# Two-layer cross-attention on one core: the first layer's scores go from one 96-row bf16 product per head to two heads in two 64-row tiles

## The reference, cut to what matters

```
q, k, v = x @ Wq + bq, ctx @ Wk + bk, ctx @ Wv + bv    # q: 32 heads of 16; k, v: 8 heads of 16
scores  = q_head . k_head * 16 ** -0.5 + mask          # 512 x 1024 for each of 32 heads
out     = softmax(scores) @ v_head
x       = layer_norm(x + out @ Wo + bo) * gamma + beta
```

## Time and profile before

| | us |
|---|---|
| median of 3 runs | 2617.61 (2616.01 to 2618.43) |
| span of the profiled execution | 2614.3 |
| TensorE busy in it | 2580.6 (99%) |
| VectorE / ScalarE / GpSimd busy | 1730.6 / 1504.9 / 1311.1 |
| granted TensorE clock | 1.000 of full speed |
| first layer's steps, batch 0: first S to the last turning of inverses | 37.8 to 289.2 |
| the same, batch 1 | 1336.9 to 1588.2 |

### The profile page before, as it was taken

How to read it: one execution, slowest core, us unless ns; L and a number is a source line. 1 busy time by engine, 2 the same in 40 slices (tenths; PEclk the granted TensorE clock), 3 DMA queues, 4 the chain that set the end, 5 groups by cost and what they waited for, 6 DMA issues and landing times.

```text
span 2614.3 us, 48985 instructions
## 1 busy us (share of the span) xinstructions
PE 2580.6 (99%) x17560; PEld 2145.5 (82%) x17560; DVE 1730.6 (66%) x2636; ACT 1504.9 (58%) x2356; POOL 1311.1 (50%) x746
## 2 busy tenths in 40 slices
PE   8999999999999999999999999999999999999999
PEld 6777788888888888888877777888888888888887
DVE  7999775656657666665279996665666576666541
ACT  5999555555545555545459994555554455554543
POOL 1244246666543666654613432466655546665644
PEclk9999999999999999999999999999999999999999
DMA  7312025345322435442472110344544143553521
GB/s 202 101 51 68 34 68 130 99 115 134 104 75 76 122 98 126 128 103 80 153 154 83 54 65 33 90 108 110 130 113 120 53 99 99 125 129 102 131 72 65
DMA packets 88386, 261.81 MB, mean 100 GB/s; under 512 B 20112, under 2 KB 33696, under 8 KB 81840
## 3 DMA queue, kind: packets, MB, share of 16 engines
q1 hardware_dynamic: 86336, 258.83, 37.3%
q10 hardware_dynamic: 1904, 0.98, 0.2%
HBM read 135.45 MB, written 6.83 MB: 54 GB/s over the span
## 4 chain that ended last, share of the span: by engine, by line
PE 88%; DVE 4%; issue 2%; ACT 2%; DMA 2%; POOL 1%; SPq 1%; DVEq 0%; POOLq 0%; ACTq 0%
PE ps_m L1059 21%; PE ps_t L1059 18%; PE ps_s L1059 15%; PE ps_m L1316 6%; PE ps_t L1316 6%; PE ps_t L1191 6%; PE ps_m L1206 5%; PE ps_s L1175 4%; PE ps_m L1191 3%; POOL pT_lo L524 1%; SPq L442 1%; PE ps_m L1249 1%; PE ps_m L1069 1%; DMA pT_lo<-pb 1%; ACT p L850 1%
## 5 line engine op out<-in xcount | busy, mean ns | idle before, releaser
L524 POOL TENSOR_TENSOR pT_lo<-pT_lo,pT_hi 128x1024 fp32r<-128x1024 f32 x220 | 529.2, 2406 | 501.7 <-ACT pT_hi L710 496.4
L710 ACT ACTIVATE pT_hi<-pT_lo 128x1024 fp32r<-128x1024 f32 x224 | 237.8, 1061 | 327.6 <-DMA pT_lo<-pb 327.6
L850 ACT ACTIVATE p<-ps_s,nm 128x1024 f32<-128x1024 f32 x256 | 284.7, 1112 | 203.4 <-DVE nm L1752 202.7
L1749 DVE TENSOR_REDUCE nmx<-ps_s 128x1 f32<-128x1024 f32 x256 | 309.7, 1210 | 121.6 <-PE ps_s L1059 121.6
L1059 PE MATMUL ps_s<-kT,qT 128*128 128x512 f32 x1536 | 383.9, 392 | 0.1
L1768 DVE STREAM_TRANSPOSE pb<-p 128x1024 f32<-128x1024 f32 x224 | 278.1, 1242 | 106.2 <-ACT p L850 101.7
L1059 PEld LDWEIGHTS ps_s<-kT,qT 128*128 128x128 f32 x1536 | 281.3, 188 | 55.6 <-ACT p L850 1.0
L1674 DVE CUSTOM_DVE_ANT_0 sm<-ps_s,mask 128x1024 f32<-128x1024 f32 x256 | 309.7, 1211 | 5.6 <-ACT p L804 2.2
L804 ACT ACTIVATE p<-sm,nm 128x1024 f32<-128x1024 f32 x256 | 293.7, 1147 | 33.3 <-DVE nm L1674 30.7
L1059 PE MATMUL ps_t<-ctxT,wa 128*128 128x512 f32 x1080 | 256.0, 390 | 0.0
L1059 PE MATMUL ps_m<-hT,wa 128*128 128x512 f32 x1008 | 243.7, 393 | 0.7 <-ACT g L1021 0.7
(11 more groups left out here) (176 smaller groups left out, 4671.7 us busy)
## 6 DMA issues: line engine op xcount, KB each, us to landing
pT_lo<-pb SPq DMA_DIRECT2D x896, 128.0 KB, 2.3
stg_qk<-in_wqk SPq DMA_DIRECT2D x40, 1024.0 KB, 7.5
stg_vo<-in_wo SPq DMA_DIRECT2D x48, 512.0 KB, 3.5
wob<-in_wo SPq DMA_DIRECT2D x32, 512.0 KB, 3.6
stg_vo<-in_wv SPq DMA_DIRECT2D x32, 512.0 KB, 3.6
q_stack<-scr_q SPq DMA_DIRECT2D x48, 128.0 KB, 4.2
st_ctx<-in_ctxT SPq DMA_DIRECT2D x8, 512.0 KB, 6.6
bv_row<-scr_bv SPq DMA_DIRECT2D x32, 128.0 KB, 5.7
```

Source lines behind the costliest of these rows:

```text
L524: return nc.gpsimd.tensor_tensor(out, x, f32(hi), ALU.subtract)
L710: return nc.scalar.activation(out, in_, ACT.Copy)
L850: nc.scalar.activation(p[t % 2][:], ps_s[t % 2][:], ACT.Exp, bias=nm[:, i:i + 1], scale=SCALE1, accum_out=sums[:, i:i + 1]).then_inc(exp_d ...
L1749: nc.vector.tensor_reduce(nmx[:, i:i + 1], ps_s[t % 2][:], AX.X, ALU.max, negate=True)\
```

## The change

Queries and keys are split into two float32r parts instead of three bf16 parts, one VectorE instruction for the second (`low_part`). Three products of parts lie on 48 rows. The even key head's rows stand at partitions 0 to 47 and the odd one's at 64 to 111, so the two heads' matmuls use two 64-row tiles of the array. A step is now even or odd in the key head: steps 2r and 2r+1 are a pair, and `scores0(r)` gives both, into `ps_s[0]` and `ps_s[1]`, when both maxima of the pair before are done. TensorE's order in loop r is T(2r), S(pair r+1), T(2r+1), two pieces of V. VectorE's and ScalarE's loops go by pairs too, and `normalised` comes after odd step 5 of a unit instead of after step 4. The order of the halves' banks becomes a pattern of eight. `v32` gets 48 columns for a head instead of 32, so that one copy serves either place in the accumulator. Values' matmuls keep their number and shape.

```diff
-Q_ORDER = (0, 0, 1, 1, 0, 2)
-K_ORDER = (0, 1, 0, 1, 2, 0)
+Q_ORDER = (0, 0, 1)
+K_ORDER = (0, 1, 0)
+TILE = 64
+PAIRS0 = STEPS0 // 2
-        q_stack = sb("q_stack", [STACK, NH0, L], BF16)
-        k_stack = sb("k_stack", [STACK, KVH, S], BF16)
-        v32 = sb("v32", [P, ST, KVH, 2 * HD], F32)
+        q_stack = sb("q_stack", [P, NH0 // 2, L], F32R)
+        k_stack = sb("k_stack", [P, KVP, S], F32R)
+        v32 = sb("v32", [P, ST, KVH, 3 * HD], F32)
-        parts = sb("parts", [P, 3, 512], BF16, 3)
+        parts = sb("parts", [P, 2, 512], F32R, 3)
-        bank_of_half = [h % 2 if h < 2 * UNIT else h % 3 for h in range(2 * STEPS0)]
+        bank_of_half = [h % 2 if h < 2 * UNIT else (0, 1, 2, 0, 2, 1, 0, 2)[h % 8] for h in range(2 * STEPS0)]
...
+        def stack_rows(e, j):
+            return slice(TILE * e + HD * j, TILE * e + HD * j + HD)
...
 # ScalarE
                 exp0(0)
                 exp0(1)
-                for t in range(STEPS0):
+                for t in range(1, STEPS0, 2):
+                    copied0(t - 1, 0)
+                    if t + 2 < STEPS0:
+                        exp0(t + 1)
                     copied0(t, 0)
                     if t + 2 < STEPS0:
                         exp0(t + 2)
 # TensorE
-                def scores0(t):
-                    kv, lt, gr = place(t)
-                    if t >= 2:
-                        pe.wait_ge(max0_done, t0 + t - 1)
+                def scores0(r):
+                    kp, lt = divmod(2 * r // UNIT, LT)
+                    if r >= 1:
+                        pe.wait_ge(max0_done, t0 + 2 * r)
                     for n in range(2):
-                        mm = nc.tensor.matmul(ps_s[t % 2][:, n * 512:(n + 1) * 512],
-                                              q_stack[:, kv * GROUPS + gr, lt * P:(lt + 1) * P],
-                                              k_stack[:, kv, n * 512:(n + 1) * 512],
-                                              start=True, stop=True)
-                    mm.then_inc(s0_filled, 1)
+                        for e in range(2):
+                            rows = slice(TILE * e, TILE * e + STACK)
+                            mm = nc.tensor.matmul(ps_s[e][:, n * 512:(n + 1) * 512],
+                                                  q_stack[rows, kp * GROUPS + r % GROUPS, lt * P:(lt + 1) * P],
+                                                  k_stack[rows, kp, n * 512:(n + 1) * 512],
+                                                  start=True, stop=True)
+                            if n == 1:
+                                mm.then_inc(s0_filled, 1)
...
-                for t in range(1, STEPS0):
-                    turned0(t)
-                    if t + 3 == STEPS0 // KVP:
-                        pe.wait_ge(stack_rest, 16 * 30 * (b + 1))
-                    if t + 3 < STEPS0:
-                        scores0(t + 3)
-                    if t >= GROUPS and t % 2 == 1:
+                turned0(1)
+                for r in range(1, PAIRS0):
+                    t = 2 * r + 1
+                    if r + 1 == PAIRS0 // KVP:
+                        pe.wait_ge(stack_rest, 16 * 30 * (b + 1))
+                    turned0(t - 1)
+                    if r + 1 < PAIRS0:
+                        scores0(r + 1)
+                    turned0(t)
+                    if t >= GROUPS:
                         for i in (t % GROUPS - 1, t % GROUPS):
                             values0(t // GROUPS * GROUPS - GROUPS, i)
 # VectorE
-                for t in range(STEPS0):
-                    if t + 2 == UNIT:
+                for t in range(1, STEPS0, 2):
+                    if t + 1 == UNIT:
                         dve.wait_ge(mask_rest, 16 * (b + 1))
                         apart()
                     if t + 2 < STEPS0:
+                        maxima0(t + 1)
+                    copied0(t - 1, 1)
+                    if t + 2 < STEPS0:
                         maxima0(t + 2)
                     copied0(t, 1)
-                    if t in (1, 3, 4):
-                        (rest_of_part, second_part, third_part)[t // 2](4)
-                    if t in (5, 7, 9):
-                        (rest_of_part, second_part, third_part)[(t - 5) // 2](5)
+                    if t in (1, 3):
+                        low_part(t // 2 + 4)
                     if t % UNIT == UNIT - 1:
                         inverse(t // UNIT)
-                    if t % UNIT == GROUPS and t > UNIT:
+                    if t % UNIT == GROUPS + 1 and t > UNIT:
                         normalised(t // UNIT - 1)
```

More of the change, by code:

```diff
@@ L344, in turned_bank, with stack_k @@
             return ps_s[c // 2][:, c % 2 * 512:(c % 2 + 1) * 512]
-        def stack_k(engine, i, kvs, done):
+        def stack_rows(e, j):
+            return slice(TILE * e + HD * j, TILE * e + HD * j + HD)
+        def stack_k(engine, i, kps, done):
             for j in range(len(K_ORDER)):
-                src = scr_k[i, :, K_ORDER[j], :].rearrange("(a e) n -> e a n", e=HD)
-                engine.dma_start(k_stack[HD * j:HD * j + HD, kvs, i * 512:(i + 1) * 512], src[:, kvs, :])\
-                    .then_inc(done, 16)
+                src = scr_k[i, :, K_ORDER[j], :].rearrange("(k e d) n -> e d k n", e=2, d=HD)
+                for e in range(2):
+                    engine.dma_start(f32(k_stack[stack_rows(e, j), kps, i * 512:(i + 1) * 512]), src[e][:, kps, :])\
+                        .then_inc(done, 16)
         @block.sync
@@ L400, in stack_q @@
                     for j in range(len(Q_ORDER)):
-                        src = scr_q[i, :, Q_ORDER[j], :].rearrange("(a e) n -> e a n", e=HD)
-                        sp.dma_start(q_stack[HD * j:HD * j + HD, i * 8:(i + 1) * 8, :], src).then_inc(done, 16)
+                        src = scr_q[i, :, Q_ORDER[j], :].rearrange("(e g d) n -> e d g n", e=2, d=HD)
+                        for e in range(2):
+                            sp.dma_start(f32(q_stack[stack_rows(e, j), i * GROUPS:(i + 1) * GROUPS, :]), src[e])\
+                                .then_inc(done, 16)
                 sp.dma_start(mask[:, 1:, :], d["mask"][b, :, 1:, :]).then_inc(mask_rest, 16)
@@ L1164, in _ @@
                 t0, u0, g0 = b * STEPS0, b * UNITS0, b * (STEPS0 // GROUPS)
-                def place(t):
-                    kp, lt = divmod(t // UNIT, LT)
-                    return 2 * kp + t % UNIT // GROUPS, lt, t % GROUPS
-                def scores0(t):
-                    kv, lt, gr = place(t)
-                    if t >= 2:
-                        pe.wait_ge(max0_done, t0 + t - 1)
-                    for n in range(2):
-                        mm = nc.tensor.matmul(ps_s[t % 2][:, n * 512:(n + 1) * 512],
-                                              q_stack[:, kv * GROUPS + gr, lt * P:(lt + 1) * P],
-                                              k_stack[:, kv, n * 512:(n + 1) * 512],
-                                              start=True, stop=True)
-                    mm.then_inc(s0_filled, 1)
+                def scores0(r):
+                    kp, lt = divmod(2 * r // UNIT, LT)
+                    if r >= 1:
+                        pe.wait_ge(max0_done, t0 + 2 * r)
+                    for n in range(2):
+                        for e in range(2):
+                            rows = slice(TILE * e, TILE * e + STACK)
[5 more added lines that the diff above has]
+                                mm.then_inc(s0_filled, 1)
                 def turned0(t):
@@ L1195, in values0 @@
                 def values0(t, i):
-                    kv, lt, _ = place(t)
                     u, e = t // UNIT, t % UNIT // GROUPS
+                    kp = u // LT
+                    cols_v = slice(0, 2 * HD) if e == 1 else slice(HD, 3 * HD)
                     if e == 0 and i == 0 and u >= 1:
@@ L1206, in values0 @@
                             mm = nc.tensor.matmul(unit0(u)[gr * 2 * HD:(gr + 1) * 2 * HD, :],
-                                                  v32[:, st, kv, :], pt0[(t + gr) % RING][:, st, :],
+                                                  v32[:, st, 2 * kp + gr % 2, cols_v], pt0[(t + gr) % RING][:, st, :],
                                                   start=e == 0 and st == 0, stop=e == 1 and st == ST - 1)
@@ L1618, in batch, with low_part @@
                 step[:] = b * DVE_B, 0
-                def rest_of_part(i):
+                def low_part(i):
                     dve.wait_ge(wide_done, b * 6 + i + 1)
                     apart()
-                    link(nc.vector.scalar_tensor_tensor(out=tmp_lo[:], in0=ps_m[i % 2][:], scalar=column0(i),
-                                                        in1=parts[i % 3][:, 0, :], op0=ALU.add, op1=sub))
+                    nc.vector.scalar_tensor_tensor(out=parts[i % 3][:, 1, :], in0=ps_m[i % 2][:], scalar=column0(i),
+                                                   in1=f32(parts[i % 3][:, 0, :]), op0=ALU.add, op1=sub)\
+                        .then_inc(part_done, 1)
```

(9 more changed lines are left out.)

38 lines of the change are left out of this document (17 added, 21 removed).

## The result

| | before | after |
|---|---|---|
| median, us | 2617.61 | 2875.67 (2875.13 to 2877.03, 3 runs) |
| ratio, 95% interval | | 1.099, 1.0972 to 1.1007 |
| span of the profiled execution | 2614.3 | 2875.2 |

The change costs 258 us. The forecast was 2808, with a range to 2845: the direction and the mechanism were foreseen, a quarter of the loss was not.

A forecast was written before the change was run, and what follows sets the result against it. TensorE was taken to bound the kernel before, VectorE close behind; after, a 4.98 us ring per pair. Span 2614.3, plus 191.6 for both batches' rings and unit waits, less 0.7, plus 3.3 to the median: 2808 us, range 2755 to 2845.

The forecast's parts named there:

- The ring: In the steps, scores, maximum, exponential, transposes, next scores close one turn a pair: 4.98 us against 3.80 before.
- S to M: Leg from the start of a pair's scores to VectorE's maximum of the even head: 0.82 us.
- T to S: Leg from the even step's eight transposes to the next pair's scores: 0.97 us, with 0.10 for the tile switch.
- M to E: Leg from VectorE's maximum to ScalarE's exponential of the even step: 1.32 us.
- The unit's wait: Values' first matmuls of a unit wait for `normalised`, starting 4.63 us after scores: 1.63 us more, for 15 units a batch.
- The clock falls: Rival: TensorE, working some 3.3 of 4.98 us a pair, drops to 1.2 GHz in the steps: about 2980 us, chance 0.05.
- once a unit a wait of 3.2 us for `aT` ahead of V: Sign expected in the profile after: TensorE idle 3.2 us before values' matmuls, once a unit.
- The head: Start of batch 0: its first scores, which waited 0.71 us for stacked queries, give back at most 0.7 us.
- The sum: Span: 2614.3 us plus 191.6 for both batches' steps less 0.7 is 2805.2; with 3.3 more, the median is 2808.5.
- TensorE's work: In the steps, TensorE's own work falls by about 0.2 to 0.4 us a pair if 64-row tiles overlap.
- the rival of 2837: The two heads' 64-row tiles run one after the other, the turn is 5.21 us: 2837 us, chance 0.12.
- The other side's 2590: Work, not waiting, sets the steps' pace; VectorE bounds at 14.36 us a unit: 27.5 us faster, 2590, chance 0.03.

The follow-up runs named there:

- e12_ahead_only: Kernel after the change, with TensorE issuing the next pair's scores ahead of both turnings of the present pair: 2717.62 us.
- e1_fill: Kernel after the change, with 16 idle transposes on TensorE ahead of the once-a-unit wait for the normalised unit: 2838.55 us.
- e10_after_mask: Kernel after the change, with the load of the mask's later rows moved behind the first stacked queries: 2870.85 us, one run.
- e7_norm_mid: Kernel after, scores ahead of both turnings, ScalarE copying before exponentials, VectorE's two maxima before its copies, normalising between the maxima: 2627.79 us, ratio 1.0039.
- e11_head: e7_norm_mid with the mask's later rows loaded after the first stacked queries and VectorE alternating maximum and copy in the first eight steps: 2611.53 us, ratio 0.9974.
- e3_norm_copy: Kernel after, normalising at the start of VectorE's loop, ScalarE copying the odd step's first half before the next even exponential: 2727.47 us.

## Why the prediction was right and where it was wrong

**The ring.** Right. It turns once a pair, through S, M, E, ScalarE's copy and T, and e12_ahead_only, which opens that ring by one moved line, brings back 158 us, some 131 of it in the units' turns at full clock. The term was 0.12 us short of 5.10: 0.09 in S to M, 0.02 in T to S and 0.01 in M to E. 126 turns of it are 15 us. The 0.09 has a source: I took the pace of the projections' float32r matmuls, 0.12 us for 256 columns, and put the even head's second matmul 0.24 us after the first; it starts 0.34 after it.

**The unit's wait.** Its length was right: V 4.74 after S where 4.63 was summed, and the turn would be 1.6 longer by it.

**The step that failed: "The clock falls".** I asked whether TensorE's share of work over a pair was too low, found 3.3 of 4.98, set it beside 12.3 of 15.5 and gave it 0.05. The clock held at that share. It fell above all in the place that another sentence of the prediction had named, "once a unit a wait of 3.2 us for `aT` ahead of V", and I did not put the two together: the sum has that wait, and nothing for the clock behind it. After 2.98 us of idleness V and the transposes behind it ran at 1.2 GHz and took some 1.6 us more, in 24 of 28 whole units and in each batch's last: 42 us. The Trainium skill (TensorE: Matmul & The Clock Gate, the two states), which the prediction cites, has half the clock for an array that has been idle; the trace agrees with it at the long wait, 0.53 of the clock in the 3.62 us behind 2.98 us of idleness, and not across the stage as I priced it. e1_fill, which fills the stall and leaves the wait, takes 1.58 us out of the unit shown. It fell in one more place, which no sentence had named: three times up to the first turning of batch 1, behind waits of at most 1.5 us, some 4 us by the comparison with e10_after_mask.

**The head.** A small term with the wrong sign. I had up to 0.7 us of gain for the earlier first scores; they came 2.8 us later, because splitting in one instruction issues the writes of the keys' parts sooner, into the load of the mask. e10_after_mask brings them back to 37.03 and is 5 us faster.

**The sum.** The span grew by 260.9, forecast 190.9. Of the 70 missing, 15 are the ring's 0.12, 42 the clock at the units' waits, 3.5 the late first scores of batch 0, about 6 what is left of the steps, of which some 4 are the fallen clock at the start of batch 1, where turns of 6 to 7 us stood (37.5 us from the first scores to the first turning, against 33.4 in batch 0), and 3.3 the stretches outside the steps (1.4 between the batches and 1.9 at the end).

**TensorE's work, and the rivals.** The saving was there and small: 0.66 us a pair for the scores instead of 0.87, and 0.10 more for the transposes ahead. Tiles overlap, so the rival of 2837 is out; their matmuls are slower than summed, as said under the ring. The other side's 2590 needed the ring open; with all rings open e7_norm_mid takes 14.91 a unit where VectorE's work was put at 14.36, and in e11_head, with the same 14.91, TensorE is at work in 221.33 of 222.0 us: it still sets the pace.

Open: why one unit's clock falls and another's does not, at the same wait, was not followed through; nor why three fell at the start of batch 1, behind shorter ones. Nor were the low clocks up to the first turnings in e1_fill to e3_norm_copy traced to one wait each.

## What to carry to other kernels

When instructions are regrouped so that a step's products come later in an in-order queue, write down the ring that closes through the other engines and its length, before counting what is saved: 0.1 to 0.2 us less work a pair came here with pairs that take 1.3 us longer. Count a long wait with what follows it: here, behind most idle stretches of 3 us, TensorE worked at half its clock for nearly all of the next 3.6. And an earlier DMA is not free: look at what large load it will now run beside.

## What the runs showed of the hardware that was not expected

Four float32r matmuls of 48 rows and 512 columns in two 64-row tiles held TensorE for 0.66 us, two of them in one tile for the same 0.66 us; in one tile the second starts 0.34 us after the first, where two bf16 matmuls of 96 rows and 512 columns start 0.22 apart. Transposes of 128 columns ahead of a switch to 64-row tiles took 0.53 us for four instead of 0.44. After 2.98 us without work TensorE ran nearly all of the next 3.6 us at 1.2 GHz, in 26 of 30 units; with a wait of 2.02 us in a unit (e12_ahead_only) the clock fell in 15 of 28. With 1.1 to 1.4 us of idleness in every 5.1 us of the steady pairs it stayed at 2.4, but it fell three times at the start of batch 1 behind waits of 0.6 to 1.5 us. Writes of 512 KB issued behind a load of 1536 KB landed in 7.6 us, and in 2.8 with that load moved away.
